# A fused attention and expert kernel: the front reordered, its root moved to GpSimd, TensorE given work from the start

## The chip, the core and the metric

The kernel runs on one core of a Trainium2 chip. The metric is the device time of one execution in microseconds (us), the median over several runs. Engines are named as in the profile: PE is TensorE, DVE is VectorE, ACT is ScalarE, POOL is GpSimd, SP is SyncE, whose queue issues most of the DMAs.

## What is computed

The input x is 4 batches of 1024 tokens with 128 features. It is layer-normed, and the normed rows go into attention with 16 heads of 8 features and into a layer of 8 experts, of which each token uses two. The output is the sum of x and both branches. The parts that matter for the change:

```
xn = (x - mean) / sqrt(var + 1e-5)
Q = rope(xn @ W_q.T);  K = rope(xn @ W_k.T);  V = xn @ W_v.T
attn = softmax(Q K.T / sqrt(8)) V @ W_o.T
scores = xn @ Wg                      (which two experts a token uses)
xhat = (xn - mean(xn)) * rsqrt(var(xn) + 1e-6)
expert e: relu(xhat*gamma+beta @ W1 + b1) @ W2 + b2
out = x + attn + xn + weighted experts
```

All numbers are fp32.

## The kernel before

The program has a **front** and 256 **steps**. The front prepares batch 0 up to the first scores. Each step `n` then does one block of 128 keys against 512 queries of four heads: PE makes the scores of step `n+1` (`scores`, L494), ACT takes their exponential in two pieces of 128x1024 (L712), PE weighs the values of step `n` with them (`weigh`, L527), and one piece of side work is hung on the step (`aside`). Side work is placed by tables of step numbers: at step 3 W_o is transposed, at step 5 the rows of gamma, beta and b1 (`turn_rows`, L540, which waits for the DMAs of L300 to L302), at steps 6 to 15 the normed rows of the later batches, and later the routing and the expert tiles. All engines run their queues in order, and semaphores tie them together.

The front, in the order in which its work is done:

- Loads of x, constants, W_q, W_k, W_v and the rotation tables. PE transposes the weights (L411, L414).
- DVE takes mean and variance of batch 0 (`moments`, L759, L762) and the root (`factors`, L766, and `rsqrt`, L743 to L750): a first guess by integer shift and three rounds of Newton, 13 small instructions on 128x8 values with the offset of L768, nearly all linked by a wait on the one before. DVE and ACT then norm four tiles each (L804, L694), PE transposes them (`turn`, L424), DVE and ACT copy the transposes out (L807, L697).
- Four **parts** in the order of `ROPE_ORDER`: (first half of the tokens, Q), (first, K), (second, K), (second, Q). For each part PE makes two projections of 512 tokens, plain and with neighbouring features swapped (L443), into one of two `sc` buffers. ACT squares the plain one (L700). DVE multiplies the swapped one with the sine (L814) and, once the square is done, the plain one with the cosine (L816), adds them (L819), and cuts off the high bits (`split_high`, L774). POOL subtracts to get the low bits (L362) and raises `low_ok`.
- SP loads the parts into **stacks**, four copies a side with 32 rows each (`load_stack`, L292): the first half of stack 0, Q and K, after `low_ok` 2; the second half after `low_ok` 4; then all of stack 1 for the next four heads; then the three rows loads and 24 loads of expert weights.
- From the squares PE and DVE work out the largest possible score (`head_norms` L457, `bound` L779, `check_bound` L462, `decide` L785 to L797). The flag that comes out (`flag_ok`) is read by PE, SP and DVE, and picks the branch in which the steps run without a shift of the exponent.
- PE projects the values of batch 0 in four pieces into `acc[0]` and `acc[1]` in turn (L433); ACT copies each out with two instructions (L704, L706).
- DVE sets both `acc` to zero (L826), takes the moments of batches 1 to 3 and their root (24 columns), and the second root for the experts (32 columns). POOL norms the 24 later tiles (L370), then scales all 32 for the experts (L377).

## Time and profile before

| what | us |
|---|---|
| median of 3 runs | 664.96 (664.7 to 665.36) |
| the profiled execution, its own time | 665.9 |
| span of that execution, first to last instruction | 664.1 |
| PE busy, all of the span | 624.2 (94%) |
| ACT busy | 508.1 (77%) |
| DVE busy | 388.1 (58%) |
| POOL busy | 202.5 (30%) |
| PE busy in the first 45 us | 26.99 |
| mean granted TensorE clock over the span | 0.985 of full |

A profile is of one execution, on the one core. Times in it count from the span's start. Busy time doesn't contain waits. An engine with a high share can still be one that waits where it matters, so the stretch at hand has to be read for itself. PEclk is the clock granted to TensorE as a share of full speed.

### The profile page before, as it was taken

What the parts mean: (1) busy time and instruction counts of PE and PEld (TensorE: products, weight loads), DVE (VectorE), ACT (ScalarE), POOL (GpSimd) and SP (SyncE); (2) the same over time, 40 slices, a digit from 0 to 9 for tenths busy, and PEclk for the clock granted to TensorE, in tenths of its full rate; (3) what the DMA queues carried; (4) which work ended last, traced back from release to release, by engine and by line L of the source; (5) the groups of instructions that cost most, each with busy time, mean ns of one, the idle gap of its engine ahead of it and who ended that gap; (6) DMA issues with size and microseconds to landing.
All of it is one profiled execution on the core that took longest, in us unless ns stands there. A gap on an engine that the chain in (4) does not pass through costs nothing.

```text
span 664.1 us, 12213 instructions
## 1 busy us (share of the span) xinstructions
PE 624.2 (94%) x4589; PEld 275.0 (41%) x4589; DVE 388.1 (58%) x1150; ACT 508.1 (77%) x551; POOL 202.5 (30%) x243
## 2 busy tenths in 40 slices
PE   3699999999999999999999999999999999999995
PEld 1224422323455555444455555544445555322222
DVE  3975568798555554587755555458775555334112
ACT  2387799888677777777777777777777777999992
POOL 0359200006763433333343343333334331100000
PEclk9979999999999999999999999999999999999997
DMA  6275702003220303100312030310032213451000
GB/s 227 52 190 175 191 1 65 1 0 79 63 60 21 92 26 75 42 17 21 88 52 62 21 92 25 75 42 17 21 88 54 60 17 80 190 188 45 1 1 34
DMA packets 25425, 43.99 MB, mean 66 GB/s; under 512 B 5472, under 2 KB 15248, under 8 KB 24848
## 3 DMA queue, kind: packets, MB, share of 16 engines
q1 hardware_dynamic: 20032, 32.15, 17.7%
q0 software_dynamic: 4608, 9.45, 5.2%
q10 hardware_dynamic: 720, 1.54, 0.6%
q8 instruction: 39, 0.64, 0.4%
q14 instruction: 26, 0.21, 0.1%
HBM read 17.43 MB, written 8.91 MB: 40 GB/s over the span
## 4 chain that ended last, share of the span: by engine, by line
PE 78%; ACT 10%; DVE 7%; issue 2%; DMA 1%; DVEq 1%; SPq 1%; POOL 0%; ACTq 0%
PE acc L527 30%; PE sc L494 18%; PE bank L579 12%; ACT ring L712 10%; PE bank L571 9%; PE bank L564 2%; PE bank L443 2%; PE bank L588 1%; DVE xn L1045 1%; PE bank L433 1%; PE bank L424 1%; DMA const<-shape_constants 1%; PE bank L555 1%; SPq L292 1%; DVEq L1042 1%
## 5 line engine op out<-in xcount | busy, mean ns | idle before, releaser
L712 ACT ACTIVATE ring<-sc 128x1024 f32<-128x1024 f32 x512 | 492.9, 1022 | 126.4 <-PE sc L494 124.9
L527 PE MATMUL acc<-ring,v 128*9 128x512 f32 x2048 | 270.5, 600 | 2.4 <-issue 2.4
L494 PE MATMUL sc<-qs,ks 32*128 32x512 f32 x1024 | 169.6, 500 | 14.2 <-ACT ring L712 9.2
L397 POOL DMA_INDIRECT token_out<-work,token x72 | 79.2, 1100 | 160.8 <-DVE work L1065 155.0
L387 POOL DMA_INDIRECT work<-normed,token x72 | 70.1, 973 | 167.9 <-DVE work L1051 91.8
L494 PEld LDWEIGHTS sc<-qs,ks 32*128 32x128 f32 x1024 | 66.2, 183 | 122.6 <-ACT ring L712 87.3
L579 PEld LDWEIGHTS bank<-xn,work 128*128 128x128 f32 x576 | 69.7, 191 | 65.1 <-issue 29.9
L1058 DVE TENSOR_SCALAR work<-bank,xn 128x128 f32<-128x128 f32 x288 | 80.9, 344 | 23.1 <-PE bank L571 23.1
L579 PE MATMUL bank<-xn,work 128*128 128x128 f32 x576 | 83.2, 287 | 3.1 <-DVE work L1051 3.1
L571 PE MATMUL bank<-work,xn 128*128 128x128 f32 x576 | 77.0, 277 | 1.4 <-DVE norms L779 1.1
L1045 DVE COPY xn<-w_all 128x1158 f32 x72 | 55.8, 776 | 33.2 <-DVE work L1065 32.3
L571 PEld LDWEIGHTS bank<-work,xn 128*128 128x128 f32 x576 | 73.1, 197 | 3.3 <-issue 1.8
L1065 DVE TENSOR_TENSOR work<-bank,xn 128x128 f32<-128x128 f32 x72 | 21.0, 291 | 78.5 <-PE bank L579 78.4
L527 PEld LDWEIGHTS acc<-ring,v 128*9 128x9 f32 x2048 | 30.4, 88 | 66.5 <-issue 65.0
L856 DVE STREAM_TRANSPOSE blocks<-acc 128x512 f32<-128x512 f32 x32 | 22.7, 710 | 53.5 <-PE acc L527 53.4
L1051 DVE TENSOR_SCALAR work<-bank,xn 128x128 f32<-128x128 f32 x72 | 29.2, 406 | 11.3 <-PE bank L564 9.3
L564 PEld LDWEIGHTS bank<-const,work 128*128 128x128 f32 x72 | 10.0, 139 | 62.3 <-issue 62.3
L564 PE MATMUL bank<-const,work 128*128 128x128 f32 x72 | 23.5, 327 | 0.3
L377 POOL TENSOR_SCALAR xn<-xn,small 128x128 f32<-128x128 f32 x32 | 18.6, 597 | 5.5 <-DVE xnT L880 5.5
L392 POOL TENSOR_SCALAR x<-x,small 128x128 f32<-128x128 f32 x32 | 16.8, 535 | 0.3
L1038 DVE TENSOR_TENSOR x<-bank,x 128x512 f32<-128x512 f32 x8 | 5.5, 692 | 18.1 <-PE bank L588 16.8
L370 POOL TENSOR_SCALAR xn<-x,small 128x128 f32<-128x128 f32 x24 | 10.5, 451 | 10.5 <-DVE small L768 10.5
(158 smaller groups left out, 311.3 us busy)
## 6 DMA issues: line engine op xcount, KB each, us to landing
qs<-hl SPq DMA_DIRECT2D x60, 128.0 KB
ks<-hl SPq DMA_DIRECT2D x60, 128.0 KB
w_all<-L_ffn_W SPq DMA_DIRECT2D x16, 256.0 KB, 4.8
x<-L_attn_x SPq DMA_DIRECT2D x4, 512.0 KB, 7.9
normed<-xn SPq DMA_DIRECT2D x4, 512.0 KB, 5.5
xn<-token_out SPq DMA_DIRECT2D x2, 1024.0 KB, 5.9
w_all<-token_out SPq DMA_DIRECT2D x2, 1024.0 KB, 10.3
out<-x SPq DMA_DIRECT2D x8, 256.0 KB, 2.2
```

The costliest lines, as they stand in the source:

```text
L387: pool.indirect_dma_start(out=xt[t % TILE_BUFFERS], out_offset=None, in_=xh_d[:, :], in_offset=bass.IndirectOffsetOnAxis(ap=token[:, 0, t: ...
L397: pool.indirect_dma_start(out=y_d[:, :], in_=ys[done % TILE_BUFFERS], in_offset=None, out_offset=bass.IndirectOffsetOnAxis(ap=token[:, 1, ...
L494: last = nc.tensor.matmul(dst, ks[r:r + 32, kb * P:(kb + 1) * P].bitcast(F32R), qs[r:r + 32, at].bitcast(F32R), start=True, stop=not slow)
L527: last = nc.tensor.matmul(acc[qh % 2][32 * j:32 * j + VW, :], v9[:, b, kb, 4 * g + j, :], ring[:, (2 * n + j // 2) % UNITS, j % 2, :], sta ...
L564: nc.tensor.transpose(bank[1][:, 0:P], xt[t % TILE_BUFFERS], ident).then_inc(bank_full[1], 1)
L571: last = nc.tensor.matmul(bank[0][:, c * P:(c + 1) * P], w_tile[t % 3][:, c * P:(c + 1) * P], xsT[t % 2], start=True, stop=True)
L579: last = nc.tensor.matmul(bank[1][:, 0:D], hT[t % 2][:, c, :], w_tile[t % 3][:, W2_AT + c * D:W2_AT + (c + 1) * D], start=(c == 0), stop=( ...
L712: nc.scalar.activation(ring[:, (2 * n + u) % UNITS, :, :], sc[u][:, :].rearrange("p (h c) -> p h c", h=2), ACT.Exp, scale=SCALE).then_inc( ...
L856: nc.vector.transpose(blocks[:, :, :].rearrange("p q r -> p (q r)"), acc[qh % 2][:, :]).then_inc(acc_out, 1)
L1045: nc.vector.tensor_copy(w_tile[t % 3], w_all[:, bass.ds(e, 1), :].rearrange("p o w -> p (o w)")).then_inc(w_ok, 1)
L1051: nc.vector.tensor_scalar(xsT[t % 2], bank[1][:, 0:P], w_tile[t % 3][:, GA_AT:GA_AT + 1], w_tile[t % 3][:, BE_AT:BE_AT + 1], ALU.mult, ALU.add
L1058: last = nc.vector.tensor_scalar(hT[t % 2][:, c, :], bank[0][:, c * P:(c + 1) * P], w_tile[t % 3][:, B1_AT + c:B1_AT + c + 1], 0.0, ALU.ad ...
```

## The change

- **Root.** POOL fills a column block with -0.5 and gets `rsqrt_of`: an addition of epsilon and a power. It is called three times: for batch 0 (8 columns), for batches 1 to 3 (24), for the experts' norm (32). DVE keeps the offset alone (`offsets`) and waits for POOL's `rstd_ok`. `rsqrt` and `factors` are gone.
- **Work on PE.** `warm` multiplies the tile of ones with itself into `sc`, whose content nobody reads: ten times before the weights' transposes and ten times behind them.
- **Parts.** `ROPE_ORDER` now has Q before K in the second half. PE projects them in the order 0 to 3, swapped one first, with a semaphore count behind each projection; part 2 goes to `acc[0]` and `acc[1]`. DVE takes them in the order 0, 1, 3, 2. The low bits of part 1 are made by DVE itself (`low_dve`).
- **First stack by halves.** SP issues the Q side after `low_ok` 1 and the K side after `low_dve`. The second half waits for `low_ok` 2 (K) and 3 (Q), the latter with a semaphore of its own, which PE asks for at step 8.
- **Decision between parts.** DVE does `bound` and `decide` behind part 1, before parts 3 and 2.
- **Values** of batch 0 go through `bank[1]` alone, one piece at a time. The zeroing of `acc` is gone; the first `weigh` waits for `rope_out` 4 in its place.

```diff
+ROPE_ORDER = ((0, 0), (0, 1), (1, 0), (1, 1))
+FRONT_ORDER = (0, 1, 3, 2)
+WARM = (10, 10)
 
...
     take(0, "bound", 0)
+    for m in range(4):
...
-            def load_stack(q, cols, landed):
+            def load_stack(q, cols, landed, sides=(0, 1)):
                 g = q % 4
-                for s in range(2):
+                for s in sides:
                     for c in range(COPIES):
                         part = c // 2 if s == 0 else c % 2
                         sp.dma_start(stack[q % 2][s][c:P:COPIES, cols], hl[32 * g:32 * g + 32, s, part, cols]
                                      ).then_inc(landed, 16)
 
+            sp.wait_ge(low_ok, 1)
+            load_stack(0, slice(0, CH), first_in, (0,))
+            sp.wait_ge(low_dve, 1)
+            load_stack(0, slice(0, CH), first_in, (1,))
             sp.wait_ge(low_ok, 2)
-            load_stack(0, slice(0, CH), first_in)
-            sp.wait_ge(low_ok, 4)
-            load_stack(0, slice(CH, S), stack_in[0])
+            load_stack(0, slice(CH, S), stack_in[0], (1,))
+            sp.wait_ge(low_ok, 3)
+            load_stack(0, slice(CH, S), later_q_in, (0,))
             load_stack(1, slice(0, S), stack_in[1])
...
-            for r in range(4):
+            nc.gpsimd.memset(small[:, 10, :], -0.5).then_inc(eps_ok, 1)
+
+            def rsqrt_of(src, dst, ts, eps, done):
+                nc.gpsimd.tensor_scalar(small[:, 9, ts], src, eps, None, ALU.add).then_inc(eps_ok, 1)
+                eps_count[0] += 1
+                pool.wait_ge(eps_ok, eps_count[0])
+                nc.gpsimd.tensor_tensor(small[:, dst, ts], small[:, 9, ts], small[:, 10, ts], ALU.pow).then_inc(done, 1)
+
+            eps_count = [1]
+            pool.wait_ge(mom_ok, 1)
+            rsqrt_of(mv[:, 0:TB, 1], 6, slice(0, TB), 1e-5, rstd_ok)
+            for i, r in enumerate(r for r in FRONT_ORDER if r != 1):
                 c, s = ROPE_ORDER[r]
                 at = slice(c * CH, (c + 1) * CH)
-                pool.wait_ge(high_ok, r + 1)
+                pool.wait_ge(high_ok, i + 1)
                 nc.gpsimd.tensor_tensor(hl[:, s, 1, at], turned[r % 2][:, :], hl[:, s, 0, at], ALU.subtract
                                         ).then_inc(low_ok, 1)
             nc.gpsimd.memset(shift[:, :], 0.0).then_inc(shift_zero, 1)
...
+            pool.wait_ge(mom_ok, B)
+            rsqrt_of(mv[:, TB:T, 1], 6, slice(TB, T), 1e-5, rstd_ok)
...
+            pool.wait_ge(xh_var, 1)
+            rsqrt_of(small[:, 5, :], 7, slice(0, T), 1e-6, xh_scale)
             pool.wait_ge(xh_scale, 1)
...
+            def warm(count):
+                for k in range(count):
+                    nc.tensor.matmul(sc[k % 2][:, 0:P], ones[:, :], ones[:, :], start=True, stop=True)
+
+            pe.wait_ge(ones_ok, 1)
+            warm(WARM[0])
             pe.wait_ge(const_in, 16)
             pe.wait_ge(wqk_in, 32)
             for k in range(2):
...
+            warm(WARM[1])
             turn(0, 0)
             turn(0, 1)
             pe.wait_ge(wT_ok, 6)
-            for r in range(4):
+            def project_front(r, plain_to, rotated_to):
                 c, s = ROPE_ORDER[r]
                 xnT_is_there(0, c)
-                wait(pe, rope_out, r - 1)
-                wait(pe, sq_ok, r - 1)
-                for k in range(2):
-                    last = project_qk(sc[r % 2][:, k * CH:(k + 1) * CH], 0, c, 2 * s + k)
-                last.then_inc(proj, 1)
+                project_qk(rotated_to, 0, c, 2 * s + 1).then_inc(proj, 1)
+                project_qk(plain_to, 0, c, 2 * s).then_inc(proj, 1)
+
+            for r in range(2):
+                project_front(r, sc[r][:, 0:CH], sc[r][:, CH:2 * CH])
+            pe.wait_ge(wvg_ok, 1)
+            project_front(2, acc[0][:, :], acc[1][:, :])
+            pe.wait_ge(rope_out, 1)
+            pe.wait_ge(sq_ok, 1)
+            project_front(3, sc[0][:, 0:CH], sc[0][:, CH:2 * CH])
             pe.wait_ge(head_ok, 1)
             head_norms(0)
-            pe.wait_ge(wvg_ok, 1)
             pe.wait_ge(gate_in, 16)
-            for m in range(2):
-                values_of(acc[m % 2], 0, m).then_inc(v_mm, 1)
+            values(0, 0)
             check_bound(0)
-            for m in range(2, 4):
-                wait(pe, v_act, 2 * (m - 1))
-                values_of(acc[m % 2], 0, m).then_inc(v_mm, 1)
-            pe.wait_ge(rope_out, 4)
+            for m in range(1, 4):
+                values(0, m)
+            pe.wait_ge(rope_out, 3)
...
                     if n == 0:
-                        pe.wait_ge(v_act, 8)
+                        pe.wait_ge(v_act, 4)
                         pe.wait_ge(v_one, 1)
-                        pe.wait_ge(acc_clear, 2)
+                        pe.wait_ge(rope_out, 4)
...
+            for r, src in enumerate((sc[0], sc[1], acc[0], sc[0])):
+                act.wait_ge(proj, 2 * r + 2)
+                nc.scalar.activation(square[0][r], src[:, 0:CH], ACT.Square).then_inc(sq_ok, 1)
             for m in range(4):
-                act.wait_ge(v_mm, m + 1)
-                src = acc[m % 2][:, 0:2 * (D + E)].rearrange("p (t c) -> p t c", t=2)
+                act.wait_ge(bank_full[1], USE["values", 0, m])
+                src = bank[1][:, 0:2 * (D + E)].rearrange("p (t c) -> p t c", t=2)
...
-                nc.scalar.copy(score[:, 2 * m:2 * m + 2, :], src[:, :, D:D + E]).then_inc(v_act, 1)
+                nc.scalar.copy(score[:, 2 * m:2 * m + 2, :], src[:, :, D:D + E]).then_inc(bank_taken[1], 1)
...
-                link(last)
-
-            def factors(ts):
-                link(nc.vector.tensor_scalar(small[:, 9, ts], mv[:, ts, 1], 1e-5, None, ALU.add))
-                rsqrt(9, 6, ts)
+                last.then_inc(mom_ok, 1)
+
+            def offsets(ts, done):
+                v.wait_ge(rstd_ok, done)
                 nc.vector.scalar_tensor_tensor(out=small[:, 8, ts], in0=mv[:, ts, 0], scalar=-1.0,
                                                in1=small[:, 6, ts], op0=ALU.mult, op1=ALU.mult).then_inc(ln_ok, 1)
...
-            factors(slice(0, TB))
+            offsets(slice(0, TB), 1)
...
+            def turn_front(i, r, plain_of, rotated_of):
                 c, s = ROPE_ORDER[r]
                 at = slice(c * CH, (c + 1) * CH)
-                v.wait_ge(proj, r + 1)
-                wait(v, low_ok, r - 1)
-                nc.vector.tensor_tensor(rotated[:, :], sc[r % 2][:, CH:2 * CH], sin[:, at], ALU.mult)
+                v.wait_ge(proj, 2 * r + 1)
+                nc.vector.tensor_tensor(rotated[:, :], rotated_of, sin[:, at], ALU.mult)
                 v.wait_ge(sq_ok, r + 1)
-                nc.vector.tensor_tensor(turned[r % 2][:, :], sc[r % 2][:, 0:CH], cos[:, at], ALU.mult
-                                        ).then_inc(rope_out, 1)
-                v.wait_ge(rope_out, r + 1)
+                nc.vector.tensor_tensor(turned[r % 2][:, :], plain_of, cos[:, at], ALU.mult).then_inc(rope_out, 1)
+                v.wait_ge(rope_out, i + 1)
                 link(nc.vector.tensor_tensor(turned[r % 2][:, :], turned[r % 2][:, :], rotated[:, :], ALU.add))
-                split_high(r).then_inc(high_ok, 1)
-                if r == 2:
-                    bound(0)
+
+            turn_front(0, 0, sc[0][:, 0:CH], sc[0][:, CH:2 * CH])
+            split_high(0).then_inc(high_ok, 1)
+            turn_front(1, 1, sc[1][:, 0:CH], sc[1][:, CH:2 * CH])
+            link(split_high(1))
+            nc.vector.tensor_tensor(hl[:, 1, 1, 0:CH], turned[1][:, :], hl[:, 1, 0, 0:CH], ALU.subtract
+                                    ).then_inc(low_dve, 1)
+            bound(0)
             decide(0)
-            v.wait_ge(v_act, 8)
-            for k in range(2):
-                nc.vector.memset(acc[k][:, :], 0.0).then_inc(acc_clear, 1)
+            v.wait_ge(low_dve, 1)
+            turn_front(2, 3, sc[0][:, 0:CH], sc[0][:, CH:2 * CH])
+            split_high(3).then_inc(high_ok, 1)
+            v.wait_ge(low_ok, 1)
+            turn_front(3, 2, acc[0][:, :], acc[1][:, :])
+            split_high(2).then_inc(high_ok, 1)
             for b in range(1, B):
                 moments(b)
-            factors(slice(TB, T))
+            offsets(slice(TB, T), 2)
             rstd = small[:, 6, :]
             v.wait_ge(ln_ok, 2)
             link(nc.vector.tensor_tensor(small[:, 5, :], mv[:, :, 1], rstd, ALU.mult))
-            link(nc.vector.tensor_tensor(small[:, 5, :], small[:, 5, :], rstd, ALU.mult))
-            link(nc.vector.tensor_scalar(small[:, 5, :], small[:, 5, :], 1e-6, None, ALU.add))
-            rsqrt(5, 7, slice(0, T), xh_scale)
+            nc.vector.tensor_tensor(small[:, 5, :], small[:, 5, :], rstd, ALU.mult).then_inc(xh_var, 1)
 
```

DVE, from the moments of batch 0 on, before (`small` holds variance, root and offset by columns, `mv` the moments; rows that repeat the Newton rounds are left out at the end):

```order
L762 BN_AGGR mv<-stats 128x2 [waits dve]
L762 BN_AGGR mv<-stats 128x2 x7
L766 TENSOR_SCALAR small<-mv 128x8 [waits dve]
L743 TENSOR_SCALAR small<-small 128x8 [waits dve]
L744 TENSOR_SCALAR small<-small 128x8
L745 TENSOR_SCALAR small<-small 128x8 [waits dve]
L748 TENSOR_TENSOR small<-small 128x8 [waits dve]
L749 TENSOR_TENSOR small<-small 128x8 [waits dve]
L750 SCALAR_TENSOR_TENSOR small<-small 128x8 [waits dve]
```

and now:

```order
L782 BN_AGGR mv<-stats 128x2 [waits dve]
L782 BN_AGGR mv<-stats 128x2 x7
L787 SCALAR_TENSOR_TENSOR small<-mv,small 128x8 [waits rstd_ok]
L823 TENSOR_SCALAR xn<-x,small 128x128 [waits ln_ok]
L823 TENSOR_SCALAR xn<-x,small 128x128 x3
L826 COPY xnT<-bank 128x512 [waits bank_full0]
```

The root's instructions have left DVE; its offset now waits for POOL.

SP's queue behind the input loads, before (`hl` holds high and low bits, `qs` and `ks` are the two sides of a stack):

```order
L292 DMA qs<-hl 32x512 [waits low_ok]
L292 DMA qs<-hl 32x512 x3
L292 DMA ks<-hl 32x512 x4
L292 DMA qs<-hl 32x512 [waits low_ok]
L292 DMA qs<-hl 32x512 x3
L292 DMA ks<-hl 32x512 x4
L292 DMA qs<-hl 32x1024 x4
L292 DMA ks<-hl 32x1024 x4
L300 DMA wr<-L_ffn_b 32x128
```

and now:

```order
L300 DMA qs<-hl 32x512 [waits low_ok]
L300 DMA qs<-hl 32x512 x3
L300 DMA ks<-hl 32x512 [waits low_dve]
L300 DMA ks<-hl 32x512 x3
L300 DMA ks<-hl 32x512 [waits low_ok]
L300 DMA ks<-hl 32x512 x3
L300 DMA qs<-hl 32x512 [waits low_ok]
L300 DMA qs<-hl 32x512 x3
L300 DMA qs<-hl 32x1024 x4
L300 DMA ks<-hl 32x1024 x4
L312 DMA wr<-L_ffn_b 32x128
```

The first four loads have a wait of their own, earlier than that of the K side, and in the second half K goes before Q.

PE, from the squares' matmuls (`head_of`) and the values (`wvg`) to the first scores, before:

```order
L457 MATMUL bank<-oT,head_of 32x512 x3
L433 MATMUL acc<-wvg,xnT 128x136 [waits gate_in,wvg_ok]
L433 MATMUL acc<-wvg,xnT 128x136 x3
L462 MATMUL bank<-const,norms 1x128 [waits bank_taken0]
L433 MATMUL acc<-wvg,xnT 128x136 [waits v_act]
L433 MATMUL acc<-wvg,xnT 128x136
L433 MATMUL acc<-wvg,xnT 128x136 [waits v_act]
L433 MATMUL acc<-wvg,xnT 128x136
L655 TENSOR_LOAD flag [waits flag_ok,rope_out]
L655 ISA x2
L658 COMPARE_AND_BRANCH
L494 MATMUL sc<-qs,ks 128x512 [waits first_in]
```

and now, from the second matmul of the first piece of the values on:

```order
L468 MATMUL bank<-wvg,xnT 128x136
L492 MATMUL bank<-const,norms 1x128 [waits bank_taken0]
L468 MATMUL bank<-wvg,xnT 128x136 [waits bank_taken1,bank_taken0]
L468 MATMUL bank<-wvg,xnT 128x136
L468 MATMUL bank<-wvg,xnT 128x136 [waits bank_taken1]
L468 MATMUL bank<-wvg,xnT 128x136
L468 MATMUL bank<-wvg,xnT 128x136 [waits bank_taken1]
L468 MATMUL bank<-wvg,xnT 128x136
L691 TENSOR_LOAD flag [waits flag_ok,rope_out]
L691 ISA x2
L694 COMPARE_AND_BRANCH
L527 MATMUL sc<-qs,ks 128x512 [waits first_in]
```

Each piece of the values now waits for ACT's copy of the piece before; before, the first two did not, and the read of the flag still stands behind all of them.

## Rows read from the trace of the kernel before

**Rows 1.** The page, part 1: busy time and instructions of each engine.

```profile
PE 624.2 (94%) x4589; PEld 275.0 (41%) x4589; DVE 388.1 (58%) x1150; ACT 508.1 (77%) x551; POOL 202.5 (30%) x243
```

**Rows 2.** Chain of waits from the start: start, length in us, engine and work.

```profile
12.19 1.97 PE bank L424 x8
...
14.18 3.15 PE sc L443 x4
...
28.06 2.08 DMA ks<-hl
30.14 0.69 issue
...
46.34 0.97 PE acc L527 x8
```

**Rows 3.** Chain of waits, steps with nothing beside them.

```profile
91.01 1.95 ACT ring L712 x2
...
94.95 1.95 ACT ring L712 x2
```

**Rows 4.** Timeline, root and norm: start, length, engine, line, work.

```profile
7.65 0.64 DVE L762 BATCH_NORM_AGGREGATE mv<-stats 128x2 f32<-128x6 f32 x8
...
11.02 1.12 DVE L804 TENSOR_SCALAR xn<-x,small 128x128 f32<-128x128 f32 x4
...
13.34 0.69 DVE L807 COPY xnT<-bank 128x512 f32<-128x512 f32 x1 [1.21 <-PE bank L424]
```

**Rows 5.** Timeline, weights' transposes, second pair's square, first high and low bits.

```profile
6.76 0.66 PE L411 MATMUL acc<-const,wr 128*128 128x128 f32 x2 [6.76 <-DMA wr<-L_attn_W_k]
...
19.06 0.60 ACT L700 ACTIVATE oT<-sc 128x512 bf16<-128x512 f32 x1 [1.12 <-PE sc L443]
...
19.47 0.43 DVE L774 TENSOR_SCALAR hl<-turned 128x512 int32<-128x512 int32 x1
...
19.98 1.27 POOL L362 TENSOR_TENSOR hl<-turned,hl 128x512 f32<-128x512 f32 x1 [18.26 <-DVE hl L774]
```

**Rows 6.** Timeline, SyncE's queue: first half stack, last short row.

```profile
23.66 2.45 SPq L292 DMA_DIRECT2D qs<-hl  x4
...
40.27 0.27 SPq L302 DMA_DIRECT2D wr<-L_ffn_beta  x1
```

**Rows 7.** Timeline, values and decision.

```profile
23.93 0.40 PE L457 MATMUL bank<-oT,head_of 128*32 128x512 bf16 x4 [0.78 <-ACT oT L700]
...
24.26 1.19 PE L433 MATMUL acc<-wvg,xnT 128*128 128x136 f32 x8
...
25.03 0.37 ACT L704 COPY v<-acc 128x256 f32<-128x256 f32 x1 [1.24 <-PE acc L433]
...
25.49 0.37 ACT L704 COPY v<-acc 128x256 f32<-128x256 f32 x1
...
29.41 0.14 DVE L797 CAST flag<-flag_f 1x1 int32<-1x1 f32 x1
```

**Rows 8.** Timeline, ScalarE's exponentials of steps 0, 1 and of step 5.

```profile
31.72 3.85 ACT L712 ACTIVATE ring<-sc 128x1024 f32<-128x1024 f32 x4 [4.52 <-PE sc L494]
...
43.85 1.94 ACT L712 ACTIVATE ring<-sc 128x1024 f32<-128x1024 f32 x2 [0.30 <-PE sc L494]
```

**Rows 9.** Windows of 2 us: busy per engine, PEclk (granted clock), DMA share, GB/s.

```profile
30.00:32.00 2.00, 0.80 (x4) 0.30 (x4) 1.95 (x10) 0.28 (x1) 0.11 (x1) 0.55 0.39 98
...
38.00:40.00 2.00, 2.00 (x16) 0.69 (x12) 1.69 (x10) 1.39 (x3) 0.00 (x0) 0.50 0.89 184
40.00:42.00 2.00, 1.93 (x12) 0.37 (x4) 1.72 (x10) 1.98 (x3) 1.43 (x4) 0.89 0.61 127
```

**Rows 10.** Timeline, VectorE behind the decision.

```profile
30.61 1.56 DVE L759 BATCH_NORM_STATS2 stats<-x 128x6 f32<-128x128 f32 x8
...
37.60 0.18 DVE L766 TENSOR_SCALAR small<-mv 128x24 f32<-128x24 f32 x1
...
44.95 0.29 DVE L868 COPY woT<-bank 128x128 f32<-128x128 f32 x1 [0.95 <-issue]
```

More of the change, by code:

```diff
@@ L439, in values @@
                 enter_bank(1, "values", b, m)
-                values_of(bank[1], b, m).then_inc(bank_full[1], 1)
+                for u in range(2):
+                    t = TB * b + 2 * m + u
+                    last = nc.tensor.matmul(bank[1][:, u * (D + E):(u + 1) * (D + E)], xnT[:, t * P:(t + 1) * P],
+                                            wvg[:, :], start=True, stop=True)
+                last.then_inc(bank_full[1], 1)
             def project_qk(dst, b, c, k):
```

57 lines of the change are left out of this document (19 added, 38 removed).

## The prediction

> **What bounds the kernel now.** Over the whole span PE is busy 94% of the time, ACT 77% [rows 1], so after the front the kernel runs at the pace of the steps, and the change doesn't touch a step. What it can move is the front and the first steps. I read the chain of waits first, then the timeline of the front, then the windows with the granted clock.
>
> The chain says which engine holds the front at each point. PE's transposes of the normed tiles start at 12.19, the first pair of projections takes 3.15 us from 14.18, the K side of the first stack lands at 30.14 (28.06 + 2.08), and the first scores start at 30.83 [rows 2]. Between these lie the root (variance ready at 8.29, first norm at 11.02) [rows 4], the rotation on DVE and the low bits on POOL, which end at 21.25 for the first part [rows 5], and SP's queue, which issues the first half from 23.66 on [rows 6]. The flag is ready at 29.55 [rows 7]. So two things end within 0.6 us of each other before the first scores: landing and flag.
>
> The clock: the second pair of projections ends 0.60 + 1.12 = 1.72 us after the first [rows 5], which itself took 3.15. PE ran at half speed until about 16.5, and before 12.19 it had done almost nothing. (The granted clock in the records still says full there; the matmuls' own times decide.) It falls again while PE stands idle ahead of the first scores: the mean is 0.55 from 30 to 32, 0.50 from 38 to 40 and 0.89 from 40 to 42 [rows 9], so it is at 1.2 GHz from just after 30 to about 40.4. Steps 0 to 4 take 43.85 - 31.72 = 12.13 us of ACT's time [rows 8], where two later steps take 94.95 - 91.01 = 3.94, or 1.97 each [rows 3].
>
> **The root.** From the variance to the norm are 2.73 us [rows 4] in 13 instructions, 0.21 each. Now: an addition and a power on POOL, three handovers, and the offset (0.21). No row has a power. Below, each POOL instruction costs what a linked small one costs on DVE, 0.21: gain 2.1. Above, each costs what a whole 128x512 pass costs on POOL, 1.27 [rows 5]: gain 0. The values are only 8 columns, so I stay near the low end: 0.9 for both with handovers. Gain 2.73 - 0.9 - 0.21 = **1.6**.
>
> One rule speaks against the move. The Trainium skill (GPSIMD Engine Reference, 2.1 Instruction dispatch) says that the first call of freshly loaded code on GpSimd pays about 6 us for the load. Nothing in this trace shows such a load ahead of POOL's first subtraction, which starts 0.08 us behind the high bits [rows 5]; if it came here, the gain by that page would be 6 us less. It is a rival below.
>
> **Work on PE from the outset.** Eight records of a projection to 136 columns, four matmuls, take 1.19 us, 0.30 a matmul at full speed [rows 7]. Ten fillers are 3.0 us, at half speed 6.0. The first ten start near 1 us and end by 7.0 at worst; the weights' transposes start at 6.76 [rows 5]. The second ten start at about 7.6 and end at 10.6 at full speed, when the tiles are normed (12.14 - 1.6 = 10.5): no delay. If the clock is up by then, the first four transposes cost half of 0.98 (eight took 1.97 [rows 2]), gain **0.5**, and the first pair 1.72 in place of 3.15, gain **1.4**. That the swapped projection comes first gives nothing: the cosine product waits for the square, and the square for the plain one.
>
> **First stack.** With 3.5 gained, the low bits of part 0 are ready at 21.25 - 3.5 = 17.75, and SP's first issue follows there and not at 23.66. The queue then sets the rest: from its first issue to the landing of the last load are 30.14 - 23.66 = 6.48 us [rows 2, 6], so 24.2. The K side isn't late: DVE ends part 0 at 19.90 - 3.5 = 16.4 [rows 5], part 1 some 2.5 later (17.33 to 19.90 for part 0), its own subtraction 0.7 later, at 19.6; the Q side is issued until 17.75 + 2.45 = 20.2.
>
> **Values and flag, what is late next.** PE's pairs start at 14.18 - 2.1 = 12.1 and end at 12.1 + 4 x 1.72 = 19.0. The last square takes 0.6, the head norms 0.4 [rows 7]: values from 20.05. A piece takes 25.03 - 24.26 = 0.77 to ACT's copy and 25.49 - 25.03 = 0.46 for the copies [rows 7]. With one bank these add up, 1.25 a piece: pieces at 20.05, 21.3, 22.55, 23.8. The flag is ready earlier: a reduction, a transpose and six small instructions behind 20.1, I estimate 22.4. But PE reads it in order, behind the last piece. That read with its branch cost at most 30.83 - 29.55 = 1.28 [rows 2, 7]; DVE stood 0.95 at the same place [rows 10]. First scores at 23.8 + 1.28, with some of the last piece's own time, **25.2**, a microsecond after the landing. Gain 30.83 - 25.2 = **5.6**. Bounds: 24.3 (landing alone) and 25.9.
>
> **Clock in the first steps.** PE works in 3.1 of the 4.4 us from 20.0 on (head norms 0.4, four pieces of 0.6 each, the check's transpose 0.3), and then waits 1 us, where before it stood still for 4.1. I expect it to stay at 2.4 GHz. Then scores to exponential take half of 31.72 - 30.83 [rows 8], and the five steps 5 x 1.97 = 9.85 in place of 12.13. Gain 0.4 + 2.3 = **2.7**, at the lower bound 0.
>
> **Rows of gamma and beta.** SP's queue got longer waits inside. Behind the decision (22.4) DVE does part 3 (24.9) and POOL its low bits (26.25); K later issues to 28.75, Q later to 31.25, stack 1 (8 loads, 5.0) to 36.25, and the last short row starts 1.2 later, at 37.5. Before it was 40.27 [rows 6]. That is 2.8 earlier, while step 5 comes 8.3 earlier: PE gets to it at 47.31 - 8.3 = 39.0 [rows 2]. The row lands at best 2.08 after its issue [rows 2], at 39.6, at worst 7.0 after it (before, PE found it landed at 47.31). I take 2.5, near a landing behind a busy queue: stall **-1.0**, bounds -0.6 and -5.5.
>
> **What costs nothing.** The zeroing of `acc` (1 us of DVE), the 26 small instructions of the two later roots (most of 37.60 to 44.0 [rows 10]): DVE has to be at W_o only when PE has done step 3, and both come earlier by about as much. If the second power takes long, that cover is gone (rival 3). The first `weigh` waits for part 2's products at about 26.2; its exponentials are there after 27.5.
>
> **Sum.** 5.6 + 2.7 - 1.0 = 7.3. The profiled execution had 665.9, so 658.6; it stood 0.94 above the median of 664.96, hence **657.7**. Bounds of the terms together: 655.5 to 662. A measurement of this kernel can tell 0.2%, 1.3 us, from no change.
>
> **Rivals.**
>
> 1. *The clock isn't held.* The fillers don't raise it by 7.6, or the thin values stage lets it fall. For it: it stayed low from 30.8 to 40.4 although PE was working in steps. Then the second ten end at 13.6 in place of 10.6, and PE's first transposes with them: gain 3.1 less, 660.8; or the first steps stay slow, 2.7 less, 660.4.
> 2. *A cheap root that isn't.* The first power pays a one-time cost of a few us, by loading or by a long start. Each us above 0.6 goes off the sum: at 3 to 6 us, 660 to 663.
> 3. *The power is dear by the column, slower than before.* Place: POOL's second call, 24 columns, ahead of `offsets`, with DVE waiting, W_o's copy and the 24 norms on POOL behind it, and PE at step 6 behind those. Moments end at 27.4 + 7.0 = 34.4 (30.61 to 37.60 before [rows 10]); step 6 comes at about 41.8, with 1.8 us of norms and 0.6 of handovers before it; slack 4.5 us. With c us a column the loss is (8c - 0.6) + (24c - 4.5), and it meets 7.3 at c = 0.39. At c = 0.5 the time is 657.7 + 3.4 + 7.5 = 668.6. Against it: POOL's plain pass costs 1.27 / 512 = 0.0025 a column [rows 5].
> 4. *The rows or the values are later.* The short rows land 5 us after issue, or the one-bank loop takes 1.7 a piece: 2 to 2.5 less, 660.
> 5. *The front wasn't the limit.* Something tied to absolute time, the expert weights or POOL's gathers, catches up: within 1 us of before. I see no such wait in the chain.
>
> **Chances.** Forecast 0.56, rival 1 0.16, rival 2 0.10, rival 3 0.05, rival 4 0.10, rival 5 0.03. The range 655.8 to 661.8 holds the forecast, rivals 1 and 4 and part of 2. Faster by over 0.2%: 0.92; within: 0.03; slower: 0.05.
>
> **What would show it.** POOL's first power under 1 us and the first norm at 9.4; the first pair at 1.7 us; the Q side's issue near 17.8; first scores near 25.2, behind the values' last piece and not a DMA; clock 1.0 from there; ACT's step 5 near 35.5; a wait of PE ahead of the rows' transpose of about 1 us. I am wrong if the first norm comes after 11, if the clock is 0.5 in steps 0 to 4, or if any step after 16 waits where none did.

## The result and the profile after

| kernel | median, us | lowest to highest | runs |
|---|---|---|---|
| before | 664.96 | 663.79 to 666.08 | 15 |
| after | 662.75 | 661.41 to 663.71 | 15 |

The ratio after to before is 0.9968, 95% interval 0.9961 to 0.9975: faster by 2.2 us. The forecast was 657.7, its range began at 655.8 and ended at 661.8, so the time lies 0.95 us above the range. The profiled execution of the changed kernel had 663.71, with a span of 661.9 and a mean granted clock of 0.982. Two executions in a slow state, one of the kernel before with 1767.9 us and one of e6 with 1780.16, are left out of every median and ratio below.

The page of the kernel after, part 1 (busy time and instructions of each engine):

```profile
PE 631.0 (95%) x4629; PEld 281.5 (43%) x4629; DVE 380.5 (57%) x1110; ACT 508.0 (77%) x551; POOL 213.1 (32%) x249
```

Against [rows 1] PE has the fillers more, DVE lost 40 instructions and 7.6 us, and POOL gained 10.6 us (its three powers alone are 11.3). None of this says where the time went. The timeline of the kernel after does (start, length, engine, line, work, idle time before and what ended it), first from the fillers to the first pair of projections:

```profile
1.04 4.63 PE L437 MATMUL sc<-ones 128*128 128x128 f32 x20 [1.04 <-DVE ones L772]
...
6.93 2.40 PE L437 MATMUL sc<-ones 128*128 128x128 f32 x20
...
7.34 0.64 DVE L782 BATCH_NORM_AGGREGATE mv<-stats 128x2 f32<-128x6 f32 x8
...
8.08 0.26 POOL L373 TENSOR_SCALAR small<-mv 128x8 f32<-128x8 f32 x1 [6.33 <-DVE mv L782]
...
8.42 1.68 POOL L376 TENSOR_TENSOR small<-small 128x8 f32<-128x8 f32 x1
...
10.34 1.12 DVE L823 TENSOR_SCALAR xn<-x,small 128x128 f32<-128x128 f32 x4
...
11.51 1.18 PE L457 MATMUL bank<-const,xn 128*128 128x128 f32 x8 [2.18 <-DVE xn L823]
...
13.04 5.37 PE L473 MATMUL sc<-xnT,wT 128*128 128x512 f32 x8 [0.35 <-DVE xnT L826]
...
16.68 0.60 ACT L736 ACTIVATE oT<-sc 128x512 bf16<-128x512 f32 x1 [3.37 <-PE sc L473]
```

The power alone takes 1.68 us. From the variance (7.98) to the norm are 2.36 us, where they were 2.73 [rows 4]. PE's second ten fillers end at 9.33 (6.93 + 2.40), and PE then stands idle for 2.18 us. The first pair of projections ends at about 16.66, 3.62 us behind its start; it took 3.15 before [rows 2].

Then from SP's first issue to the first scores, the same view:

```profile
20.57 2.45 SPq L300 DMA_DIRECT2D qs<-hl  x4
...
23.07 8.26 SPq L300 DMA_DIRECT2D ks<-hl  x8
...
25.00 0.14 DVE L816 CAST flag<-flag_f 1x1 int32<-1x1 f32 x1
...
26.97 1.24 PE L468 MATMUL bank<-wvg,xnT 128*128 128x136 f32 x4 [0.63 <-ACT score L742]
...
28.14 0.80 PE L527 MATMUL sc<-qs,ks 32*128 32x512 f32 x4
...
29.05 3.85 ACT L748 ACTIVATE ring<-sc 128x1024 f32<-128x1024 f32 x4 [0.35 <-PE sc L527]
...
41.18 3.77 ACT L748 ACTIVATE ring<-sc 128x1024 f32<-128x1024 f32 x4 [0.43 <-PE sc L527]
```

The first half is issued 3.1 us earlier than in [rows 6] and the flag is there 4.4 us earlier than in [rows 7]. The first scores come 2.7 us earlier (28.14 for 30.83), behind the last piece of the values and behind no DMA. That piece starts at 26.97 and takes 1.24 us at half speed, where the three before it take 0.70 to 0.73. Its half speed isn't what the scores wait for: in e8 (below) it takes 0.70, and the scores start 1.14 us behind its start there, 1.17 here. Steps 0 to 4 take 41.18 - 29.05 = 12.13 us, to the hundredth what they took before [rows 8].

Why these steps gained nothing is in the windows of the kernel after: the stretch, busy time of PE, PEld, DVE, ACT and POOL, PEclk (granted clock), DMA share, GB/s:

```profile
12.00:14.00 2.00, 1.65 (x8) 0.89 (x7) 0.69 (x1) 0.58 (x1) 0.00 (x0) 0.80 0.12 38
14.00:16.00 2.00, 2.00 (x4) 0.88 (x3) 0.69 (x1) 0.00 (x0) 0.00 (x0) 0.50 0.00 0
16.00:18.00 2.00, 2.00 (x5) 0.84 (x4) 0.69 (x1) 0.60 (x1) 0.00 (x0) 0.85 0.00 0
...
24.00:26.00 2.00, 1.15 (x8) 0.92 (x8) 1.74 (x8) 0.61 (x4) 0.00 (x0) 1.00 0.39 103
26.00:28.00 2.00, 1.37 (x7) 1.09 (x6) 1.93 (x4) 0.45 (x2) 0.36 (x1) 0.71 0.13 35
28.00:30.00 2.00, 0.94 (x5) 0.29 (x4) 1.93 (x5) 1.40 (x4) 0.91 (x1) 0.50 0.01 4
...
36.00:38.00 2.00, 2.00 (x16) 0.68 (x12) 0.58 (x8) 1.39 (x3) 1.25 (x2) 0.73 0.76 191
```

The clock falls to 1.2 GHz twice in these stretches. The first time is at about 13.2, behind the pause from 9.3 to 11.5, and lasts until about 16.6: it takes in the first pair. The second is at about 26.8. PE hadn't stood still for more than 0.8 us at a time then, but from 24 to 26 it was busy for only 1.15 us of 2. It is back at about 37.

Step by step (start of PE's weighing of the values), the two kernels keep the distance of 2.6 to 2.8 us from step 0 to step 168. Then 0.6 is lost once, at step 169, and the last step is 2.26 earlier. The loss is in one copy of expert weights on DVE, which comes later behind DVE's work and takes longer. Timeline, the kernel after:

```profile
447.09 1.01 DVE L1069 COPY xn<-w_all 128x1158 f32 x1 [0.81 <-DVE work L1089]
```

and the kernel before:

```profile
449.41 0.77 DVE L1045 COPY xn<-w_all 128x1158 f32 x1 [0.46 <-DVE work L1065]
```

### The profile page after: what moved, and what is told of

Read it like the earlier page. It is cut to its first block, busy times and chain, and to the rows that moved or that the text cites. A ratio compares the mean times of both kernels' runs of the same rounds, so it can differ in the third digit from the quotient of the medians.

```text
span 661.9 us, 12273 instructions
## 1 busy us (share of the span) xinstructions
PE 631.0 (95%) x4629; PEld 281.5 (43%) x4629; DVE 380.5 (57%) x1110; ACT 508.0 (77%) x551; POOL 213.1 (32%) x249
## 4 chain that ended last, share of the span: by engine, by line
PE 79%; ACT 11%; DVE 6%; issue 2%; DMA 1%; DVEq 1%; POOL 0%; ACTq 0%
PE acc L560 30%; PE sc L527 18%; PE bank L612 12%; ACT ring L748 11%; PE bank L604 9%; PE bank L597 2%; PE bank L473 2%; PE bank L621 1%; PE bank L468 1%; DVE xn L1069 1%; PE sc L473 1%; PE bank L588 1%; DMA const<-shape_constants 1%; PE bank L457 1%; DVE blocks L880 1%
## 5 line engine op out<-in xcount | busy, mean ns | idle before, releaser
L527 PE MATMUL sc<-qs,ks 32*128 32x512 f32 x1024 | 169.5, 500 | 10.5 <-ACT ring L748 9.7
L597 PE MATMUL bank<-const,work 128*128 128x128 f32 x72 | 23.5, 327 | 0.3
L468 PE MATMUL bank<-wvg,xnT 128*128 128x136 f32 x64 | 11.6, 306 | 2.1 <-ACT score L742 1.5
```

Of the source, the lines that this page charges most:

```text
L527: last = nc.tensor.matmul(dst, ks[r:r + 32, kb * P:(kb + 1) * P].bitcast(F32R), qs[r:r + 32, at].bitcast(F32R), start=True, stop=not slow)
L597: nc.tensor.transpose(bank[1][:, 0:P], xt[t % TILE_BUFFERS], ident).then_inc(bank_full[1], 1)
```

## Experiments

They ran in three batches (e1 to e4, e5 to e8, e9 to e12), each beside the kernel before, whose median was 664.78 to 665.02 in them. Diffs are cut, and are against the changed kernel unless it says otherwise. A single profile shows a single course of the clock, so a verdict goes by the medians, and a profile says what happened in one execution.

### e1: all three roots back on VectorE

The helper `rsqrt` is the one of the kernel before; the second and third root go back in the same way.

```diff
-            pool.wait_ge(mom_ok, 1)
-            rsqrt_of(mv[:, 0:TB, 1], 6, slice(0, TB), 1e-5, rstd_ok)
...
-                v.wait_ge(rstd_ok, done)
+                link(nc.vector.tensor_scalar(small[:, 9, ts], mv[:, ts, 1], 1e-5, None, ALU.add))
+                rsqrt(9, 6, ts)
```

> The changed kernel with all three roots back on VectorE (13 linked small instructions each); all else as changed. Theory A (the power on GpSimd gives almost nothing: 2.36 us from variance to first norm against 2.73 before): 0.4 us slower than the changed kernel, 663.1, the front otherwise the same. Theory B (my forecast: the move is worth 1.6 us): 664.3. Theory C (the second power, 4.20 us for 24 columns, is what costs later): faster than the changed kernel, 662.3 or less.

Measured: 662.5, ratio 0.9967 (0.9955 to 0.998). From variance to norm its profile shows 2.73 us, 0.37 more than the kernel after. Moving the root is worth nothing that this kernel's median shows.

The traces show where the 0.37 us can go. The loss of 0.6 us at step 169 stands in the profiled execution of each of the ten kernels with the roots on GpSimd (after, e2 to e9, e11): the copy there comes 0.81 or 0.82 us behind DVE's work and takes 1.01. It stands in none of the four with the roots on DVE (before, e1, e10, e12): 0.46 and 0.76 or 0.77. Why the place of the roots changes that copy isn't shown.

### e2 and e3: no fillers; nineteen behind the weights' transposes

```diff
-WARM = (10, 10)
+WARM = (0, 0)      e2
+WARM = (10, 19)    e3
```

> The changed kernel without the twenty matmuls of ones; all else as changed. Theory A (the clock they raise is lost again before the projections, so they only speed the transposes): within 0.5 us of the changed kernel, 662.7 to 663.3; the first pair of projections takes 3.2 to 3.6 us in both. Theory B (forecast: they are worth 1.9 us): 664.7.

> The changed kernel with 19 in place of 10 matmuls of ones behind the weights' transposes, so that TensorE works until the normed tiles are there (6.9 to 11.5 us). Theory A (the clock fell in the pause from 9.3 to 11.5): granted clock 1.0 at 13 us, first pair 1.7 us in place of 3.6, everything up to the first scores 1.9 us earlier, 660.9, the first steps still at half speed. Rival: the clock falls anyway, in another pause: no change, 662.8.

Measured: e2 663.77, ratio 0.9979 (0.9968 to 0.999); e3 661.81, ratio 0.9955 (0.9938 to 0.9972). The three levels stand in order, 0.9979, 0.9968, 0.9955, about 1 us apart, though the intervals touch. The timeline of e3:

```profile
7.27 5.87 PE L437 MATMUL sc<-ones 128*128 128x128 f32 x38
...
12.98 1.04 PE L457 MATMUL bank<-const,xn 128*128 128x128 f32 x8
```

The first pair took 2.0 us, where it takes 3.62 in the kernel after. But the nineteen fillers ended only at 13.14, and held PE's turn up, which could have begun at 11.6. So the first scores came at 28.00, just 0.14 us earlier. Most of what this execution gained came behind them: the clock held until about 30.8 and was back at 34.3, and steps 0 to 4 took 11.24 us in place of 12.13. More fillers helped, then, but not by the way that I expected: the pair's gain was spent on the late turn.

### e4: two fillers behind each values piece

They write to `sc[1]`, which PE waits for once ahead of the first.

```diff
+HOLD = 2
...
+                warm(HOLD, 1)
```

> The changed kernel with two matmuls of ones behind each of the four pieces of batch 0's values, in the pause in which TensorE waits for ScalarE's copy. Theory A (the clock fell at 26.8 because TensorE worked in only about half of the values' stage): clock 1.0 through the first steps, the last piece 0.6 us shorter and the first five steps 9.9 us in place of 12.1, together 2.9 us less: 659.9. Rival 1 (only the pause ahead of the first scores matters): clock falls as before, no change or 0.3 slower, 662.8 to 663.1. Rival 2 (the first five steps are held by ScalarE or DMA, not by the clock): clock held, but under 1 us gained.

Measured: 661.86, ratio 0.9954 (0.9942 to 0.9967), 0.9 us less than after. The windows of e4 (columns as above):

```profile
24.00:26.00 2.00, 1.82 (x14) 1.66 (x15) 1.86 (x8) 0.45 (x2) 0.00 (x0) 1.00 0.40 102
...
28.00:30.00 2.00, 0.79 (x6) 0.18 (x2) 1.93 (x5) 1.62 (x2) 0.89 (x2) 1.00 0.07 14
...
32.00:34.00 2.00, 2.00 (x12) 0.31 (x10) 1.97 (x15) 1.84 (x3) 0.22 (x1) 0.63 0.29 73
```

The clock lives through the values, with PE busy 1.82 of 2 us, and falls later, at about 32.5. Ahead of that lies the pipeline's start, where PE works 0.79 of 2 us (28 to 30). I read this as a second thin place behind the first. In e3 the clock also passed the values, without these fillers, so one execution doesn't show that the fillers held it.

### e5: the first stack not by halves

```diff
-            load_stack(0, slice(0, CH), first_in, (0,))
...
-            load_stack(0, slice(0, CH), first_in, (1,))
+            load_stack(0, slice(0, CH), first_in)
```

> The changed kernel with the first stack loaded in one go: SyncE waits for the low bits of both sides, then issues all eight loads. Issue would start at 22.3 in place of 20.6 and the last load land at 28.8 in place of 27.1. Theory A (the first scores at 28.1 stand only 1.1 us behind the landing): the landing becomes the bound, first scores near 28.9, 0.7 us slower than the changed kernel, 663.5. Rival (values and flag read bound the first scores with more room than that): no change, 662.8.

Measured: 661.66, ratio 0.9959 (0.9944 to 0.9973), 1.1 us less than after, where I expected more. The timeline of e5 shows the landing late all the same:

```profile
20.98 2.44 SPq L300 DMA_DIRECT2D qs<-hl  x4
...
27.51 0.53 PE L526 MATMUL sc<-qs,ks 32*128 32x512 f32 x4 [1.30 <-DMA ks<-hl]
```

PE waits 1.30 us for the K side, as theory A had it. But in this execution the first pair ran at full clock (two pairs, eight matmuls, in 3.67 us for 5.37), so SP's issue came only 0.41 us later than in the profile of after. The clock then fell at about 27.9 and was back 6.8 us later, where the kernel after was without it for 10.2. Whether the median is so for the same reason the run can't say. As it stands e5 doesn't tell the halves' worth; e11 does.

### e6: the decision behind all parts

The bound and the decision go behind the last part's high bits on DVE, and PE's transpose for the bound behind all four pieces of values.

```diff
-            bound(0)
-            decide(0)
...
+            bound(0)
+            decide(0)
...
-            check_bound(0)
...
+            check_bound(0)
```

> The changed kernel with the decision behind all four parts on VectorE (and its transpose on TensorE behind all four pieces of values), so that only its place is undone. Theory A (the place of the decision carries the gain that is left): flag at 29.4 in place of 25.1, first scores 1.2 later at 30.6, 2.5 us slower than the changed kernel, 665.2, no gain on the kernel before. Rival (landing and halves carry it): at most 1 us slower, 663.8.

Measured: 665.42, ratio 1.0007 (0.9997 to 1.0017), 2.7 us more than after and all of its gain. The timeline of e6:

```profile
18.89 2.45 SPq L300 DMA_DIRECT2D qs<-hl  x4
...
28.15 0.14 DVE L815 CAST flag<-flag_f 1x1 int32<-1x1 f32 x1
29.64 0.80 PE L526 MATMUL sc<-qs,ks 32*128 32x512 f32 x4 [2.40 <-issue]
```

SP issues here 1.7 us earlier than in the kernel after, and it helps nothing: the flag is ready at 28.29, 3.15 us later than in the kernel after, and PE stands at it. The place of the decision is the part that the rest needs. How much of the 2.7 us is the flag alone isn't shown: the clock was at 1.2 GHz from about 23.5 to 37.3 in this execution, and the eleven executions lie in two groups, five at 664.0 to 664.9 with a mean clock of 0.984 to 0.989, six at 665.4 to 666.1 with 0.982 or 0.983.

### e7: values from two banks

```diff
+            def value_home(b, m):
+                return sc[1] if b == 0 and m % 2 == 0 else bank[1]
```

Every second piece of the values goes into half of a score buffer.

> The changed kernel with the values of batch 0 in two places in turn (a half of the second score buffer, free after part 1, and the bank as now). Theory A (the first scores wait for the last piece of the values, made in a loop of 1.33 us a piece): last piece near 25, first scores at the landing, 27.1 in place of 28.1, 1.0 us faster than the changed kernel, 661.8; the clock may still fall. Rival (TensorE's clock alone makes the last piece late): 0.5 us or less gained.

Measured: 662.73, ratio 0.997 (0.9959 to 0.998): no gain. The timeline of e7:

```profile
22.70 8.20 SPq L300 DMA_DIRECT2D ks<-hl  x8
...
27.05 0.51 PE L535 MATMUL sc<-qs,ks 32*128 32x512 f32 x4 [1.52 <-DMA ks<-hl]
```

The values end sooner, and PE then waits 1.52 us. The view names the K side, whose last load landed at 26.70. The read of the flag, which also needs the third part's cosine product (ready at 25.95), may have ended later. From the head norms to the first scores 4.85 us pass, where the kernel after has 5.52, so the one bank does cost 0.67 us there. The clock falls at about 28.6 behind the pause, steps 0 to 4 are as slow as ever (12.14 us), and the median shows no gain.

### e8: fillers in all three thin places

Four more ahead of the turn, two behind each piece of values, five behind the scores of step 0.

```diff
-WARM = (10, 10)
+WARM = (10, 14)
+HOLD = 2
+FIRST_FILL = 5
...
+                fill(HOLD, sc[1])
...
+                    if n == -1 and not slow:
+                        fill(FIRST_FILL, bank[0])
```

> The changed kernel with matmuls of ones in every pause of the front: 14 in place of 10 behind the weights, two behind each piece of the values, five between the first scores and their exponential. Theory A (the clock costs what is missing, and each pause lets it fall): the two gains of 0.9 us seen with one pause filled add up and the first steps run at full speed throughout, 660.0 to 660.5. Rival (the two measures gain the same time, since only the clock in the first steps matters): 661.8.

Measured: 659.66, ratio 0.9923 (0.9907 to 0.9938): 3.1 us less than after, 5.1 less than before. It has the lowest median of all (e9 is level with it). The windows of e8:

```profile
12.00:14.00 2.00, 1.56 (x11) 1.11 (x10) 0.69 (x1) 0.72 (x2) 0.00 (x0) 1.00 0.16 52
...
24.00:26.00 2.00, 1.63 (x13) 1.37 (x12) 1.93 (x4) 0.62 (x4) 0.00 (x0) 1.00 0.27 72
26.00:28.00 2.00, 2.00 (x19) 1.58 (x18) 1.97 (x4) 1.06 (x3) 1.28 (x1) 1.00 0.04 12
28.00:30.00 2.00, 1.65 (x14) 0.90 (x16) 1.97 (x9) 2.00 (x3) 1.16 (x1) 1.00 0.22 52
30.00:32.00 2.00, 2.00 (x16) 0.49 (x12) 1.97 (x16) 1.83 (x3) 1.24 (x3) 1.00 0.41 106
```

and its timeline:

```profile
25.65 0.70 PE L474 MATMUL bank<-wvg,xnT 128*128 128x136 f32 x4 [0.18 <-ACT score L753]
...
26.79 0.50 PE L536 MATMUL sc<-qs,ks 32*128 32x512 f32 x4
...
27.39 3.77 ACT L759 ACTIVATE ring<-sc 128x1024 f32<-128x1024 f32 x4 [0.55 <-PE sc L536]
...
35.87 4.20 POOL L378 TENSOR_TENSOR small<-small 128x24 f32<-128x24 f32 x1
...
39.31 0.27 SPq L316 DMA_DIRECT2D wr<-L_ffn_beta  x1
...
41.69 0.29 DVE L903 COPY woT<-bank 128x128 f32<-128x128 f32 x1 [0.81 <-issue]
41.82 0.26 PE L582 MATMUL bank<-const,wr 48*128 48x48 f32 x1 [0.98 <-DMA wr<-L_ffn_beta]
```

The granted clock is 1.00 in all of these, past the start of the steps, and steps 0 to 4 take 9.98 us in place of 12.13. (It was at 0.50 from about 7.3 to 10.7 in this execution, so that the fourteen fillers ran until 12.11 and held the turn up by about 0.3 us.) The products of step 0 come 4.63 us earlier than in the kernel before, those of step 3 6.48 earlier: the first steps give back 1.85 more. Then PE waits 0.98 us for the row of beta, as the forecast's last term had it, and 1.06 of the distance is gone by step 7. Later 0.3 is lost at step 66, 0.26 at step 130 and 0.6 at step 169. At 661.34 this execution was the slowest of the six, with the lowest mean clock, 0.989; the fastest had 658.53 with 0.998.

### e9: e8 with two banks

Against e8:

```diff
+            def value_home(b, m):
+                return sc[1] if b == 0 and m % 2 == 0 else bank[1]
...
+                fill(HOLD, sc[1][:, CH:2 * CH])
```

> e8_filled with the values in two places in turn. With the clock held, the first scores stand at 26.8, behind the last piece of the values; the last load would land near 25.8. Theory A (values' loop is the bound at the held clock): first scores near 25.9, 1.0 us faster than e8_filled, 658.7. Rival (the pause that opens ahead of the first scores lets the clock fall, as it may have in e7): no faster than e8_filled, 659.7.

Measured: 659.84, ratio 0.9927 (0.9914 to 0.9941): level with e8. In its profile the first scores start at 27.24, behind a wait of 1.67 us for the K side. But the last K load took 3.57 us to land there, where it takes 2.07 to 2.10 in all other profiles but e11's; with 2.1 it would have been there at 25.7, 1.5 us sooner. So this trace can't say what the two banks give, and the median shows nothing.

### e10: e8 with the roots on VectorE

Against e8:

```diff
-            rsqrt_of(mv[:, TB:T, 1], 6, slice(TB, T), 1e-5, rstd_ok)
...
+                rsqrt(9, 6, ts)
```

> e8_filled with all three roots back on VectorE. Theory A (the power costs 0.42 us and 0.16 a column, so that the move gives back what it saves): within 0.5 us of e8_filled, 659.3 to 660.2. Theory B (the root on GpSimd gains once the clock is out of the way): 1 us or more slower, 660.7. Theory C (the second and third power hold later work up): 1 us faster, 658.7.

Measured: 660.71, ratio 0.9938 (0.9925 to 0.9951), 1.05 us more than e8, though the intervals touch. The timeline of e10, for the same places:

```profile
43.18 0.29 DVE L915 COPY woT<-bank 128x128 f32<-128x128 f32 x1 [0.93 <-issue]
43.61 0.63 PE L452 MATMUL bank<-const,xn 128*128 128x128 f32 x4 [0.87 <-DVE woT L915]
```

Steps 0 to 3 stand as in e8. But with the small instructions of the second root on DVE its copy of W_o comes 1.5 us later, and PE waits for it ahead of the next turn (0.87). That cover, which I had priced at nothing, is thin once the front is fast. By step 8 e10 is 0.38 us behind e8. But it doesn't have the loss of 0.6 at step 169, and in the end its profiled execution is the faster one (660.62 for 661.34). That the power earns something here rests on the medians alone, and isn't shown.

### e11: e8 without the halves

Against e8:

```diff
-            load_stack(0, slice(0, CH), first_in, (0,))
...
+            load_stack(0, slice(0, CH), first_in)
```

> e8_filled with the first stack loaded in one go, after the low bits of both sides. e5 could not tell, because the clock differs from execution to execution. Theory A: issue starts 1.7 later, the landing becomes the bound, near 27.5 in place of first scores at 26.8, 0.7 us slower than e8_filled, 660.4. Rival (halves give nothing): 659.7.

Measured: 661.91, ratio 0.9961 (0.9948 to 0.9975), 2.25 us more than e8. The timeline of e11:

```profile
21.00 2.44 SPq L302 DMA_DIRECT2D qs<-hl  x4
...
28.93 0.80 PE L535 MATMUL sc<-qs,ks 32*128 32x512 f32 x4 [2.25 <-DMA ks<-hl]
```

The halves bring SP's issue forward by 1.70 us (19.30 in e8). Without them PE waits 2.25 us for the K side, and the clock falls at about 28.7 in that pause. Of this wait 1.4 us belong to this execution: its last K load took 3.49 us to land, and not 2.1. What is left, about 0.8, is the landing's share that I had expected. That the halves are worth something is shown, as the intervals of e8 and e11 don't touch; that the clock in such a pause makes up the rest of the 2.25 us is likely, but a single profile with a late load doesn't show it.

### e12: the kernel before, with fillers alone

Fourteen behind the values, ahead of PE's wait for the last rotation, and five behind the scores of step 0.

```diff
+            pe.wait_ge(ones_ok, 1)
+            fill(14, bank[1])
...
+                    if n == -1 and not slow:
+                        fill(5, bank[1])
```

> The kernel before with nothing but matmuls of ones: fourteen behind the values of batch 0 and five between the first scores and their exponential. Theory A (the clock's fall ahead of the first scores costs 2.3 us in the first five steps and 0.4 in the first score): clock 1.0 from 26 to 45, first scores still at 30.8, 2.4 us faster than before, 662.5, as much as the whole change gives. Rival (the first five steps are held by something else): under 1 us, 664.2.

Measured: 662.97, ratio 0.997 (0.9959 to 0.9981): 2.0 us less than before, as much as the whole change within the intervals. The windows of e12:

```profile
28.00:30.00 2.00, 1.42 (x13) 1.23 (x12) 1.74 (x6) 0.00 (x0) 1.70 (x3) 1.00 0.36 89
30.00:32.00 2.00, 1.59 (x14) 1.36 (x14) 1.97 (x12) 0.99 (x2) 0.00 (x0) 1.00 0.41 105
34.00:36.00 2.00, 2.00 (x20) 0.49 (x12) 1.93 (x15) 1.83 (x3) 0.00 (x0) 1.00 0.44 107
```

Its first scores come at 30.41, only 0.42 us earlier than before, but the clock is 1.00 where it was 0.55 from 30 to 32 and 0.50 later [rows 9], steps 0 to 4 take 9.98 us in place of 12.13, and by step 5 it is 2.87 us ahead.

## Why the prediction was wrong

The sign and the path were right, the size was more than three times too large: 7.3 us forecast, 2.2 measured. The terms, a gain with a plus, against the profiled execution:

| term | forecast | measured | difference |
|---|---|---|---|
| root, variance to norm | +1.6 | +0.37 | -1.2 |
| transposes at full clock | +0.5 | +0.46 | 0 |
| first pair | +1.4 | -0.47 | -1.9 |
| first scores, all of the front | +5.6 | +2.7 | -2.9 |
| clock in the first steps | +2.7 | 0 | -2.7 |
| rows of gamma and beta | -1.0 | 0 | +1.0 |
| later in the span | 0 | -0.4 | -0.4 |

The fourth line contains the three above it. The transposes' term is from the turn's start to the first projection, 1.53 us for 1.99. Of the 2.7 us of the front, 0.3 is that x landed earlier in this execution. What the front gains beyond the first pair's end was forecast at 2.1 and measured at 2.0. The last line is the 0.6 of step 169, of which 0.17 comes back at the very last step.

**The root was mis-sized.** The step "I stay near the low end: 0.9 for both with handovers" took the smallest neighbour for an operation of which no row existed. Addition, power and handovers took 2.15 us, from 7.98 to 10.13, where 0.9 was forecast. The three powers took 1.68, 4.20 and 5.46 us for 8, 24 and 32 columns:

```profile
L376 POOL TENSOR_TENSOR small<-small x3: 1680/4197/5457, 8.4 to 52.5; 128x8 f32<-128x8 f32 x1, 128x24 f32<-128x24 f32 x1, 128x32 f32<-128x32 f32 x1
```

(The kernel after, the line of the power: shortest, median and longest in ns.) That is (5.457 - 1.680) / 24 = 0.157 us a column and 0.42 beside it. The first power alone is above the 1.27 us that the forecast had as its upper bound for one instruction; a plain pass bounds no power. So the power is dear by the column, which was rival 3's condition, but at 0.16 and not above 0.39 it stays short of the rival's point: the second power, 4.20 us, fits its slack of 4.5. Rival 2's one-time cost doesn't exist here: the first addition on POOL starts 0.10 us behind the variance and takes 0.26, and the three powers lie on one line. The Trainium skill (GPSIMD Engine Reference, 2.1 Instruction dispatch) puts about 6 us on the first call of freshly loaded code. Nothing in this trace shows such a load.

**The first pair stood on "If the clock is up by then".** The ten fillers were priced at 3.0 us, with their end at 10.6, next to the turn at 10.5. They took 2.40 and ended at 9.33, and the turn came at 11.51, since the root was slower. Both errors widen the same pause, and the clock fell behind it, so that the pair took 3.62 us and not 1.72. That the pause is the cause is likely, and not shown. Of the six profiled kernels with ten fillers there, four lost the clock before or in the first pair (after, e1, e4, e7, with pauses of 2.16 to 2.71 us). e5 kept it behind a pause of 2.24, and in e6 the fillers ran slower and left a pause of 0.43. Of the five with fourteen or nineteen none lost it there (e3, e8 to e11). The medians of e2 and e3 lie 1 us above and 0.9 below that of the kernel after, but e3's trace puts its gain elsewhere.

**"I expect it to stay at 2.4 GHz" failed, and it was the largest error.** It was argued from busy time, 3.1 of 4.4 us. In the event PE worked 1.15 of 2 us in the values, the clock fell at 26.8 before the first scores, and the first steps ran as slow as ever. That is the second form of rival 1, which I gave 0.16 with its other form. The other form didn't come as written: the fillers did raise the clock by 6.93 (0.24 us each, for 0.46 at first). It was lost again behind them, which no rival had. What shows this cause is that it can be undone: e12 adds nothing but fillers to the kernel before, its steps 0 to 4 take 9.98 us and it gains 2.0; e8 does the same in the changed kernel, with 9.98 again, and gains 3.1, of which its fillers ahead of the turn may have a share. In e4 the clock passed the values and fell in the pipeline's start. In e8 the gain of steps 0 to 3 was 1.85 us with the wait for the rows behind it 0.98, near the forecast's 2.3 and -1.0: those terms were right for a front that the change alone doesn't reach.

**What held.** The landing isn't the limit, the last values piece is; the first scores start 1.17 us behind that piece's start, the read of the flag included; without the decision's new place 2.7 us are lost (e6). The small instructions of the later roots cost nothing where they were, in this kernel (e1); with e8's front the second root holds PE up once, by 0.87 us (e10). The zeroing was taken back in no run. The rows' wait didn't come because step 5 came 2.7 us earlier and not 8.3. The upper bound of 662 was too low for the bounds that it was to sum up: 4.9 for the front, 0 for the clock and -5.5 for the rows give 665.6, so the range left less room than the terms did.

**What stays open.** Why the copy at step 169 is slower in every profiled kernel with the roots on GpSimd, and in none of the others. Losses of 0.25 to 0.45 us at steps 66, 130 and 194 appear in some profiles and not in others. Nor is it settled how often the clock's fall takes in the first pair in the kernel after: its fifteen times spread over 2.3 us, with mean clocks of 0.981 to 0.990, and one of them is profiled.

## What to carry to other kernels

A clock term isn't won by raising the clock once: list every place up to the steady state where the engine is thin or idle, and either fill all of them or count the gain as nothing. Fillers that end too early leave a pause, and fillers that run too long hold up the work behind them, as in e3. For an operation of which no row exists, neighbours of another kind give no bounds: here even the upper one was too low for the power. Before a reordering of a front, try the cheap half alone: a few lines of fillers in the old kernel (e12) gave as much as the whole reordering, and the two together (e8) 5.1 us, somewhat more than the sum of 4.2. And look into a single profile for what belongs to that execution alone, as the late load in e11, before its waits are taken for the change's price.

## What the runs showed of the hardware

- A power on GpSimd costs 0.42 us and 0.157 us a column of 128 fp32 values; a plain pass there costs 1.27 us for 512 columns [rows 5], 0.0025 a column.
- The clock can fall to 1.2 GHz although TensorE never pauses for more than 0.8 us: in the kernel after it fell at 26.8, and TensorE was busy 1.15 of 2 us from 24 to 26. It need not: in e3 and e5 the same pieces of values, with the same pauses, ran at full clock to their end.
- The mean granted clock of an execution goes with its time: e8's six executions go from 0.989 (661.34 us) to 0.998 (658.53).
- The point of a change of level differs from one execution to the next of kernels with the same front: the first two pairs took 5.37 us in after, 3.67 in e5 and e6. These are 1.7 us apart, and one profile shows one course of the clock. The Trainium skill (TensorE: Matmul & The Clock Gate, Part 1) says that the number of slow matmuls at the start of the same kernel differs from run to run. No kernel is profiled twice here; kernels with the same front agree with it.
- A load from SBUF to SBUF of 32x512 fp32 values took 2.06 to 2.13 us from issue to landing on the K side of the first half, and once 3.57 (e9) and once 3.49 (e11).
- A fp32 matmul of 128 columns shows as two records and took 0.24 us at 2.4 GHz (2.40 us for ten fillers).
